# The gate of a gated linear-attention recurrence from its two thin factors, in column and row tiles of the matmul engine

## What is computed

```python
probs = softmax(x @ w_gate)                      # 4 memories, each token goes to the top 2
tx = the tokens of each memory, 256 at most for each of 8 sequences
q, k, v = tx @ w_q * scale, tx @ w_k[m], tx @ w_v[m]         # 128, 128 and 256 wide
gk = tx @ w_gk1[m] @ w_gk2[m] + b_gk[m]          # 256 -> 16 -> 128
gk = log_sigmoid(gk) / 16
S = S * exp(gk_t) + k_t v_t^T;  o_t = q_t S      # the recurrence, 4 heads
# the same once more for all tokens with shared weights (w_ks, w_vs, w_gk1s, w_gk2s, b_gks)
o = (rmsnorm(o_routed + o_shared) * norm_w) * silu(x @ w_g) @ w_o
```

## Time and profile before

| | |
|---|---|
| time, median of 3 runs | 802.96 us (799.78 to 806.54) |
| span of the profiled execution | 760.2 us |
| the median less the span | 42.8 us |
| TensorE matmul / weight load busy | 92% / 81% of the span |
| VectorE, ScalarE, GpSimd busy | 66%, 46%, 33% |
| stretch 36 to 53 us (end of the first stage) | TensorE busy 15.5 of 17 us |
| stretch 53 to 115 us (slots 0 to 2) | TensorE busy 58.4 of 62 us |
| stretch 115 to 246 us | TensorE busy 122.8 of 131 us |
| stretch 246 to 421 us | TensorE busy 175.0 of 175 us |

### The profile page before, as it was taken

The page is one execution under the profiler, slowest core; times in us unless marked ns, Lnnn a source line. Parts: engine busy times, 40 slices in busy tenths (PEclk is TensorE's granted clock), DMA queues, the critical chain, the costliest instruction groups (busy, mean ns, idle before and its releaser), DMA issues.

```text
span 760.2 us, 25608 instructions
## 1 busy us (share of the span) xinstructions
PE 695.7 (92%) x11058; PEld 618.6 (81%) x11058; DVE 501.5 (66%) x1159; ACT 348.2 (46%) x765; POOL 247.4 (33%) x358
## 2 busy tenths in 40 slices
PE   7998998999989999999999999508999999999993
PEld 6886787989978999899899888407689998999992
DVE  6716774555446678777767677678378878877820
ACT  2663544445544546655656564530353345325410
POOL 5510044555644413223140431001734253203333
PEclk9998999999999999999999998755899999999997
DMA  7960024343443635454544453720735255312213
GB/s 201 391 276 2 31 99 153 109 135 124 157 149 112 196 96 158 135 165 140 168 109 142 138 164 108 262 49 3 233 130 154 54 156 139 120 21 28 29 21 36
DMA packets 75467, 96.81 MB, mean 127 GB/s; under 512 B 11337, under 2 KB 67057, under 8 KB 74202
## 3 DMA queue, kind: packets, MB, share of 16 engines
q1 hardware_dynamic: 62250, 69.52, 28.0%
q0 software_dynamic: 12288, 25.12, 13.2%
q10 hardware_dynamic: 816, 0.53, 0.2%
HBM read 53.78 MB, written 41.55 MB: 125 GB/s over the span
## 4 chain that ended last, share of the span: by engine, by line
PE 78%; DVE 10%; issue 4%; DMA 3%; POOL 2%; ACT 1%; POOLq 0%; DVEq 0%
PE bank L1828 41%; PE attn L1828 27%; PE bank L1786 3%; PE bank L1880 2%; DVE arena L1488 2%; PE bank L1887 1%; DMA arena<-x_p,idxs 1%; PE attn L2189 1%; DMA big<-o_m,gidx 1%; DVE st L1043 1%; PE attn L1771 1%; PE attn L1990 1%; POOL arena L524 1%; POOL big L467 1%; DVE big L1056 1%
## 5 line engine op out<-in xcount | busy, mean ns | idle before, releaser
L1828 PE MATMUL attn<-arena 32*32 32x64 f32 (+4 forms) x6048 | 140.3, 225 | 9.2 <-issue 7.3
L1828 PE MATMUL bank<-xT,arena 128*128 128x128 f32 (+2 forms) x964 | 145.8, 306 | 0.0
L1828 PEld LDWEIGHTS attn<-arena 32*32 32x32 f32 (+3 forms) x6048 | 114.2, 120 | 33.2 <-issue 15.4
L1828 PEld LDWEIGHTS bank<-xT,arena 128*128 128x128 f32 x964 | 124.3, 192 | 11.2 <-issue 5.8
L467 POOL DMA_INDIRECT big<-o_m,gidx x64 | 71.0, 1109 | 159.7 <-PE bank L1828 116.9
L460 POOL DMA_INDIRECT x_c<-big,sidx x64 | 68.6, 1071 | 119.3 <-PE bank L1828 88.9
L1828 PE MATMUL bank<-arena,xT 128*128 128x128 f32 (+2 forms) x640 | 107.1, 320 | 0.1
L1828 PEld LDWEIGHTS bank<-arena,xT 128*128 128x128 f32 x640 | 90.0, 199 | 8.6 <-issue 2.9
L543 POOL DMA_INDIRECT out_dram<-arena,idxs x32 | 50.2, 1569 | 109.6 <-ACT arena L1010 99.3
L1165 DVE COPY_PREDICATED arena<-causal,attn 128x1024 f32<-128x1024 int32 x24 | 31.6, 1316 | 71.2 <-PE attn L1828 71.2
L524 POOL DMA_INDIRECT arena<-x_p,idxs x32 | 34.3, 1070 | 98.8 <-DVE idxs L1567 70.8
(11 more groups left out here) (305 smaller groups left out, 1249.2 us busy)
## 6 DMA issues: line engine op xcount, KB each, us to landing
x_c<-zeros SPq DMA_DIRECT2D x8, 1024.0 KB, 9.2
xT<-x_c SPq DMA_DIRECT2D x16, 512.0 KB, 4.1
o_m<-arena SPq DMA_DIRECT2D x16, 512.0 KB, 4.0
xT<-in_L_ffn_W_dram SPq DMA_DIRECT2D x8, 1024.0 KB, 7.9
gs<-in_L_ffn_W_dram SPq DMA_DIRECT2D x8, 1024.0 KB, 7.6
xT<-in_L_attn_x_dram SPq DMA_DIRECT2D x8, 512.0 KB, 5.2
out_dram<-xT SPq DMA_DIRECT2D x8, 512.0 KB, 5.2
arena<-in_L_attn_x_dram SPq DMA_DIRECT2D x7, 512.0 KB, 6.2
```

The lines of the kernel that those rows point to most:

```text
L1828: return nc.tensor.matmul(out_, l, r, start=a, stop=z, skip_group_check=True)
```

## The change

The matrix `wz` and both preparations go. SyncE now loads `w_gk1` as it is (`wlow`), `w_gk2` four times, at partitions 0, 32, 64 and 96 (`wup`), and the biases as columns (`bcol`); these ten transfers stand ahead of the loads of `w_q`, `w_k` and `w_v`. The gate of a group becomes three steps: `low_rank(g)`, eight matmuls, each with 16 columns of weights and 128 tokens, tile j to partitions 32j to 32j+15 of bank 5; `low_in(g)`, one ScalarE copy to `low`; `gate(g)`, four matmuls with 16 rows of weights, tile j from partitions 32j on, to the first 128 columns of bank j (`gates`, the banks of the scores and outputs).

With it the order changes. The values are computed one tile at a time (`values(s,0)` to `values(s,3)`), the keys stand ahead of the outputs of the group before, the updates use banks 4 and 6, and the scores follow the second half of the row transposes. Waits are added so that the shared banks are free: `gate` for `masked` of two groups before, `outputs` and `scores` for `gate_in`, `updates` for the copy of the second half of the rows. The number for the gate leaves `SPANS`; the others stay.

```diff
--- before.py
+++ after.py
@@ -110,6 +110,7 @@
         attn = ctx.enter_context(nc.psum_tensor("attn", [P, 4, 512], F32))
+        gates = attn[:, :, 0:P]
...
@@ -197,9 +198,11 @@
-        wz = dv("wz", [P, NS, 2, P])
+        wlow = dv("wlow", [P, NS, 2, LOW])
+        wup = dv("wup", [P, NS, P])
...
+        low = dv("low", [P, P])
...
@@ -578,6 +574,12 @@
+            for j in range(TB):
+                at = slice(32 * j, 32 * j + LOW)
+                sp.dma_start(wup[at, 0:M, :], w_gk2.rearrange("m r n -> r m n")).then_inc(wl_in, 16)
+                sp.dma_start(wup[at, SHARED, :], w_gk2s).then_inc(wl_in, 16)
+            sp.dma_start(bcol[:, 0:M], b_gk.rearrange("m n -> n m"), allow_slow_non_contiguous=True).then_inc(wl_in, 16)
+            sp.dma_start(bcol[:, SHARED:NS], b_gks.rearrange("(n a) -> n a", a=1)).then_inc(wl_in, 16)
...
@@ -706,31 +708,10 @@
-            def low_rank_t():
-                act.wait_ge(w_tp, 1)
...
-            def merged_gate():
-                act.wait_ge(w_mm, 1)
...
@@ -750,6 +731,12 @@
+            def low_in(g):
+                act.wait_ge(d_l, g + 1)
+                if g >= 1:
+                    act.wait_ge(d_z, g)
+                nc.scalar.activation(low[:, :], bank[5][:, 0:P], ACT.Copy).then_inc(d_lc, 1)
...
@@ -889,10 +876,13 @@
+            low_in(0)
             softplus(0)
             decays(0)
             for s in range(NG):
...
+                if s + 1 < NG:
+                    low_in(s + 1)
                 values(s, 0)
...
@@ -1148,14 +1138,17 @@
             def gate_in(g):
                 dve.wait_ge(d_z, g + 1)
...
-                z = bank[4]
+                y = ybuf[:, :].rearrange("p (j t) -> p j t", j=TB)
                 if not routed(g):
-                    ins = nc.vector.tensor_scalar(ybuf[:, :], z, bcol[:, SHARED:SHARED + 1], None, ALU.add)
+                    ins = nc.vector.tensor_scalar(y, gates, bcol[:, SHARED:SHARED + 1], None, ALU.add)
...
@@ -1177,7 +1170,7 @@
-                    u = bank[5 + c % 2][:, CH * (c // 2):CH * (c // 2) + CH]
+                    u = bank[4 + 2 * (c % 2)][:, CH * (c // 2):CH * (c // 2) + CH]
...
@@ -1838,42 +1808,52 @@
+            def low_rank(g):
                 if routed(g):
                     pe.wait_ge(d_xt, 2 * (g - FIRST) + 2)
-                if g >= 1:
-                    pe.wait_ge(d_y, g)
-                if g == 3:
-                    pe.wait_ge(r_read, 1)
-                channels(bank[4], lambda m: wz[:, m, :, :], g, SPANS[g - 1][1] if g else S).then_inc(d_z, 1)
+                for k in range(2):
+                    for j in range(TB):
+                        ins = mm(bank[5][32 * j:32 * j + LOW, 0:P], wlow[:, memory(g, j), k, :],
+                                 columns(g, k, P * j, P * j + P), k == 0, k == 1)
+                ins.then_inc(d_l, 1)
+
+            def gate(g):
+                pe.wait_ge(d_lc, g + 1)
+                if g >= 2:
+                    pe.wait_ge(d_am, g - 1)
+                for j in range(TB):
+                    r = slice(32 * j, 32 * j + LOW)
+                    ins = mm(gates[:, j, :], wup[r, memory(g, j), :], low[r, :])
+                ins.then_inc(d_z, 1)
 
             def keys(g):
-                if g >= 1:
-                    pe.wait_ge(d_t, g)
...
             def rows_t(g, k):
                 n = g - FIRST
                 if k == 0:
                     pe.wait_ge(d_in[n % 2], 16 * (n // 2 + 1))
-                    pe.wait_ge(d_y, g)
+                    pe.wait_ge(d_t, g - 2)
                 else:
                     pe.wait_ge(d_xt, 2 * n + 1)
...
             def scores(g):
                 pe.wait_ge(d_qd, g + 1)
+                pe.wait_ge(d_y, min(g + 2, NG))
...
             def updates(g):
                 pe.wait_ge(d_kt, g + 1)
                 pe.wait_ge(d_qd, g + 1)
+                if g == 1:
+                    pe.wait_ge(r_read, 1)
+                if routed(g + 2):
+                    pe.wait_ge(d_xt, 2 * (g + 2 - FIRST) + 2)
                 pe.wait_ge(d_vs, 2 * g + 2)
...
-                            ins = mm(bank[5 + c][r, CH * j:CH * j + CH], kt[s, j, r],
+                            ins = mm(bank[4 + 2 * c][r, CH * j:CH * j + CH], kt[s, j, r],
...
             def outputs(g):
                 pe.wait_ge(d_t, g + 1)
                 pe.wait_ge(d_am, g + 1)
+                pe.wait_ge(d_y, min(g + 3, NG))
...
@@ -2060,18 +2046,23 @@
-            gate(0)
+            low_rank(0)
             pe.wait_ge(a_gs, NT)
             pe.wait_ge(a_lg, NT)
+            gate(0)
             for s in range(NG):
+                if s + 1 < NG:
+                    low_rank(s + 1)
                 values(s, 0)
+                if s == 0:
+                    pe.wait_ge(d_y, 1)
                 if s + 1 < NG:
                     gate(s + 1)
+                values(s, 1)
+                keys(s)
                 if s >= 1:
                     outputs(s - 1)
-                if s < NG:
-                    keys(s)
-                    queries(s)
+                queries(s)
...
                     keys_t(s)
-                    values(s, 1)
+                    values(s, 2)
...
                     if routed(s + 2):
                         rows_t(s + 2, 0)
-                    scores(s)
+                    values(s, 3)
                     if routed(s + 2):
                         rows_t(s + 2, 1)
+                    scores(s)
```

108 lines of the change are left out of this document (35 added, 73 removed), and 10 rows, old and new, of the table SPANS.

## The result

The changed kernel takes 868.83 us (median of 4 runs, 861.16 to 872.85) against 801.37 us (798.71 to 806.54) for the kernel before: 1.086 times as long, 95% interval 1.082 to 1.090. I had forecast 818 us, 804 to 840. The sign was right; the loss is 67 us instead of 15.

A forecast was written before the change was run, and what follows sets the result against it. Prediction: TensorE bounds the kernel, with VectorE's chain as long in a slot. Terms -5.4 + 9.3 + 3.1 - 1.2 + 6 x 0.9 + 10 x 0.7 - 2.9 = +15.3 us put the 802.96 median at 818, range 804 to 840.

The forecast's parts named there:

- to the first `updates`: First stage and slot 0: dropped preparations save 5.4 us; late `low_in`, slow clock and slower products cost 9.3.
- slot 1: `gate(2)` waits for `decays(1)`, so `keys_t(1)` comes later; with the slow clock, 3.1 us lost.
- slots 2 to 4: Each of these slots gains 0.4 us, 1.2 us in all.
- slots 5 to 10: Slots without woven work: the chain beside TensorE sets the length, 15.9 us against 15.0, 0.9 lost in each.
- slots 11 to 20: Woven work hides the chain but not the wait for `group_out`: 0.7 us lost in each slot.
- slots 21 to 23: No row transposes: 0.6 us gained each, and a 1.11 us wait for `states` goes, 2.9 in all.
- The thin products: New gate on TensorE, tiles side by side: 1.0 us a slot with edges instead of 1.88, a gain of 0.9.
- The rival without overlap: Thin products do not run side by side: 1.9 us a slot instead of 0.46, +28 us, 846 us; chance 0.08.
- The wait of `rows_t`: End of slots 5 to 20: second row transposes wait for `rows_in`, 1.27 us idle, 1.43 lost each.
- The middle of a slot: From `updates` to `keys_t`, the chain through `masked`, `states` and `gate_in` takes 9.64 us.
- The start: Slots 0 and 1: `gate(1)` and `gate(2)` wait for late `low_in` copies, some 6 us each, slow clock behind.
- the clock falls too: Rival: the clock falls in each of 16 slots, 1.5 us each, +24 us, 842 us; chance 0.13.

The follow-up runs named there:

- e5: The changed kernel run and profiled again as it is, at the upper level: 1.092 of the kernel before.
- e11: The kernel before, unaltered, profiled again at the upper level: 804.15 us, ratio 1.000.
- e4: The kernel before with the last value tile between the row transposes and the second row transposes ahead of the scores: 1.037 of before.
- e1: The changed kernel with the second half of the row transposes written to bank 6 instead of bank 4: 1.067 of the kernel before.
- e3: The changed kernel with 64 short products (128 instructions) added in slot 0 ahead of `gate(1)`: 840.4 us, 1.099 of the kernel before.
- e16: The kernel of e17 with the second row transposes in the middle of the scores instead of ahead of them: 765.1 us, 1.000 of before.
- e9: The changed kernel with only `SPANS` altered, so most slots from 3 on have as many TensorE records as before: 1.065 of the kernel before.
- e7: The kernel before with two unused thin blocks a slot, behind the updates and ahead of the gate: 1.039 of before.
- e12: The kernel before with 8 unused 32-column products (16 instructions) behind the updates of each slot: 1.021 of before.
- e17: The changed kernel with bank 6, the copy ahead of the decays, record counts of before and early `low_in`: 785.7 us, 1.027 of before.

## Why the prediction was right in sign and wrong in size

By stages, at one level, e5 less e11, beside the terms of my sum:

| stage | forecast | measured |
|---|---|---|
| to the first `updates` | -5.4 + 9.3 = +3.9 | +1.2 |
| slot 1 | +3.1 | +6.9 |
| slots 2 to 4 | -1.2 | +6.3 |
| slots 5 to 10 | +5.4 | +7.5 |
| slots 11 to 20 | +7.0 | +41.1 |
| slots 21 to 23 | -2.9 | +3.1 |
| behind | 0 | +1.0 |
| sum | +15.3 | +67.1 |

No rival reached the result either: the longest, 846 us, is 23 us short of it.

*The thin products.* Right. In the recorded execution at the upper clock `low_rank` takes 0.56 us from start to start (72.22 to 72.78) and `gate` 0.43 (50.23 to 50.66): 0.99 us with their edges, 1.0 forecast. The 16 thin records start in fours, the four within 21 ns. The rival without overlap (1.9 us for the thin records alone) is out, and with it what I had drawn from the Trainium skill (TensorE: Matmul & The Clock Gate, The mechanism): the four thin tiles share all row groups and still run side by side. In slots 11 to 20 the work at full speed, with idle time at half speed counted once, falls from 175.2 to 167.0 us, 0.8 a slot for the 0.9 forecast.

*The wait of `rows_t`.* Right in cause and place. Its shortest form, 1.18 us of idle time, stands in six or seven of the 16 slots (1.27 forecast); in the others it is 1.4 to 2.9 us long, and the 16 come to 24.3 us in the recorded execution and 27.5 in e5, where 16 x 1.27 = 20.3 were forecast. e4 shows the cost of the wait alone (28 us on the kernel before, 16 x 1.43 = 22.9 forecast).

*The middle of a slot.* The forecast 9.6 us from the updates to `keys_t` of slot 7 is met in e5 (9.6), not in the recorded execution (13.5), where the first half of the slot runs at half speed.

*The start.* Right in sum (7.0 us forecast, 8.1 measured), but by luck: the first part is 2.7 us less than forecast and the second 3.8 more. `gate(1)` and `gate(2)` wait as said, with a slow clock behind:

```profile
58.17 0.81 PE L1798 MATMUL attn<-arena 16*128 16x128 f32 x8 [5.79 <-ACT arena L739]
...
79.51 0.81 PE L1798 MATMUL attn<-arena 16*128 16x128 f32 x8 [5.59 <-ACT arena L739]
```

*What failed, first: the clock, a term put at nothing in the forecast and kept as a rival, "the clock falls too".* I gave it 0.13, 16 slots and 1.5 us a slot, because the clock had stayed up behind 1.11 us of idle time in slot 23. Measured: 94.6 us more at half speed over 23 slots, which cost 43 to 47 us, about 2 us a slot. e4 shows that a wait of that size among full-array products leaves the clock up. In e1 it falls behind single waits of 0.8 us between scores and updates in slots 8 to 10, so the one wait that I looked at could not stand for the others. A second stop in the slot does not decide it: in slot 7 of e4 TensorE idles 3.4 us and in slot 10 of e3 3.8, both at full speed throughout. What decides in which slot the clock falls stays open.

*Second, a term that was missing: the stops without a releaser.* I took the few of before as given. In slots 11 to 20 they grow from 3.2 us to 12.9, and the waits for `rows_in` from 0.6 to 16.2. Idle time there goes from 5.4 to 30.4 us and half-speed time from 4.5 to 56.7; idle time makes +25.0, the clock +24.4 and the work -8.2 (idle time at half speed counted once), together +41.1 against +7. Two parts of the change bear on them. It put scores and updates, 176 records and as many weight loads, in one piece, and transposes in the middle of the scores win 20.6 us (e16). It dropped the gate's number from `SPANS` and left the others, which gave most slots 8 records more; with the counts put right 0.021 to 0.027 of the time is won (e9).

*Third, the frame.* I took 42.8 us for what lies around a span; it was the distance between two levels of the kernel. It didn't move the forecast, since I added a difference to the median, but it hid that the profile I read had fewer stops than the runs I was to predict: at the upper level products into `attn`, most of them scores, stop 39 times between 70 and 500 us, 21.3 us in all (e11):

```profile
PE attn L1828 <- issue: 21.3, 39, 1.2
```

A sign of both failed terms was in the trace that I had: the stop of 2.72 us in slot 4 with slow products behind it.

## What to carry to other kernels

Where one engine is busy 175 of 175 us, new idle time can cost more than its length: here 39 us of it came with 43 us lost to the slow clock. It need not: in e4 24 us more of idle time cost 3 us of clock. Count a saving on the array only after every wait and stop that the new order makes is gone; each of four small mends of order (bank and copy, two early copies, widths, four transposes) was worth about as much as the whole saving. A table of widths that was fitted to one order of instructions is part of that order: take out an entry, and the number of instructions per slot has to be put right. Where an engine stops without a releaser, count its instructions: equal distances of 256 here named the cause that the waits did not.

## What the runs showed of the hardware

Between the first and the last `updates` of the 19 profiles the clock fell 234 times. In 233 cases TensorE had stood idle for 0.68 us or more, in all, in the 8 us ahead. The exception is e16 at 455.39 us: 0.08 us of idle time in 12 us, the last 2.8 us being scores and then products of 8 columns. So idle time goes with the falls, but is not needed for each. 32 narrow records more in a slot did not bring the clock down in slots 13 to 20 of e7, five of which have no stop at all; in slots 8 to 10 of e1 it fell each time behind a single stop of 0.8 us inside narrow work.

The stops without a releaser are of two kinds. Number all of TensorE's records in a trace in order of time, from 0, and 242 of these stops in the 19 profiles (over 0.15 us, those of `rows_t` left out) stand in front of record 193 or 194 of a block of 256, in every version of the kernel. In e3 the stops of slots 7 to 13 stand in front of records 5825, 6594, 7361, 8130, 8897, 9666 and 10434, three blocks apart. The page of before has 22116 TensorE instructions (matmuls and loads), and these transfers of instructions (packets, MB, share of the DMA engines):

```profile
PE 695.7 (92%) x11058; PEld 618.6 (81%) x11058; DVE 501.5 (66%) x1159; ACT 348.2 (46%) x765; POOL 247.4 (33%) x358
...
q8 instruction: 87, 1.43, 0.8%
```

16.4 KB each, one for 254 instructions. Each of the 242 stops ends 1.1 to 1.7 us after such a transfer has ended; an arbitrary moment of the recurrence lies so in one case of ten. In slot 9 of e3 the transfer runs from 214.92 to 216.32 and the stop, 2.27 us long, ends at 217.80. So TensorE waits here for its own instructions. The Trainium skill (Advanced Engine Details and Errata, Sequencer and Instruction Queues) says that a line of the instruction cache is 16 KB, 256 instructions, that there are only two, and that the cache has 128 KB on TensorE; size and count of the line agree with the trace, and how many lines TensorE holds no run here shows.

Stops of this kind grow where narrow work is dense or the counts drift. Over the recurrence they take 1.9 us in e11 and 12.7 in e12, with 16 instructions a slot more; 24.9 us in e17 and 13.2 in e16, with four transposes inside the scores. In slots 13 to 21 of before (recorded) a slot has 767 matmul and load instructions on average, three blocks, and the stops are absent; the changed kernel has some 20 more. Why a transfer comes too late in one slot and not in another stays open.

The second kind is short, 1.3 us at most but for two, stands at other places in the stream, and all but four of its 407 stops lie in products into `attn`. It goes with the two levels: the 12 profiles at the upper level have 24 to 44 each (e11: 38, 21.0 us), the seven at the lower level one of 0.16 us together. Its cause stays open; an instruction transfer takes 1.0 to 1.1 us (the medians of the profiles) at both levels.
